# Graph attention layers of a GNN and expert kernel: masks by ScalarE ahead of the first layer, logit sums by half tiles, GpSimd's low parts behind each head

## The reference

```python
def gat_layer(x, W, att_src, att_dst, bias, src, dst, heads, out_ch, concat):
    h = (x @ W.T).reshape(n, heads, out_ch)
    a_src = jnp.einsum('nhc,hc->nh', h, att_src)
    a_dst = jnp.einsum('nhc,hc->nh', h, att_dst)
    e = jax.nn.leaky_relu(a_src[src] + a_dst[dst], 0.2)
    m = jax.ops.segment_max(e, dst, num_segments=n)
    ex = jnp.exp(e - m[dst])
    denom = jax.ops.segment_sum(ex, dst, num_segments=n)
    alpha = ex / (denom[dst] + EPS)
    out = jax.ops.segment_sum(alpha[:, :, None] * h[src], dst, num_segments=n)
    return out + bias
h = gat_layer(x, W1, ..., heads=8, out_ch=128)
out = gat_layer(relu(h), W2, ..., heads=1, out_ch=768)
```

## Time and profile before

| | |
|---|---|
| median of 3 runs | 1395.59 us (1395.35, 1395.59, 1403.01) |
| the profiled execution's own time | 1399.6 us |
| its span | 1397.6 us |
| mean granted TensorE clock | 0.95 |
| busy: PE, PEld, DVE, ACT, POOL | 1248.6, 1063.9, 922.0, 578.2, 133.5 us |
| TensorE's share of the span | 89% |

### The profile page before, as it was taken

The page is one execution under the profiler, slowest core; times in us unless marked ns, Lnnn a source line. Parts: engine busy times, 40 slices in busy tenths (PEclk is TensorE's granted clock), DMA queues, the critical chain, the costliest instruction groups (busy, mean ns, idle before and its releaser), DMA issues.

```text
span 1397.6 us, 18195 instructions
## 1 busy us (share of the span) xinstructions
PE 1248.6 (89%) x6471; PEld 1063.9 (76%) x6471; DVE 922.0 (66%) x1765; ACT 578.2 (41%) x1005; POOL 133.5 (10%) x127
## 2 busy tenths in 40 slices
PE   5999999999999899998788999999985867878876
PEld 3577579879889786657788999999984667765643
DVE  4478664375365564556659999999987679647313
ACT  2121232432522423353148889888871255211110
POOL 0000200000000000033020000000020185010101
PEclk9999999999999999998699999999998979988799
DMA  9420280501402600040468999999984000020286
GB/s 343 146 91 30 102 305 12 204 0 47 169 1 86 232 0 0 1 158 0 147 238 308 386 392 394 382 399 387 386 307 180 27 1 1 1 79 1 100 302 229
DMA packets 82907, 229.72 MB, mean 164 GB/s; under 512 B 5217, under 2 KB 18593, under 8 KB 82721
## 3 DMA queue, kind: packets, MB, share of 16 engines
q1 hardware_dynamic: 74944, 191.96, 37.2%
q0 software_dynamic: 7904, 36.97, 7.2%
HBM read 202.18 MB, written 26.74 MB: 164 GB/s over the span
## 4 chain that ended last, share of the span: by engine, by line
PE 73%; DVE 14%; DMA 5%; issue 3%; ACT 2%; POOL 2%; SPq 0%; ACTq 0%; DVEq 0%; POOLq 0%
PE dve_ps L727 11%; PE dve_ps L729 11%; PE dve_ps L728 11%; PE act_ps L727 4%; PE act_ps L729 4%; PE act_ps L728 4%; PE dve_ps L770 4%; PE dve_ps L816 3%; DMA slot<-in_e1w 2%; PE dve_ps L960 2%; PE act_ps L943 2%; PE act_ps L767 2%; PE act_ps L816 1%; PE dve_ps L1202 1%; DVE part_slot L2100 1%
## 5 line engine op out<-in xcount | busy, mean ns | idle before, releaser
L2091 DVE TENSOR_TENSOR part_slot<-slot,item_hi 128x768 fp32r<-128x768 f32 x150 | 133.5, 957 | 0.4 <-ACT item_hi L1541 0.2
L1541 ACT ACTIVATE item_hi<-slot 128x768 fp32r<-128x768 f32 x156 | 118.0, 834 | 27.8 <-DMA slot<-in_e0w 23.2
L2100 DVE TENSOR_TENSOR part_slot<-slot,item_hi 128x768 fp32r<-128x768 f32 x132 | 116.6, 954 | 0.4
L1549 ACT ACTIVATE item_hi<-slot 128x768 fp32r<-128x768 f32 x132 | 99.3, 833 | 9.0 <-DMA slot<-in_e0w 9.0
L727 PE MATMUL dve_ps<-item_hi,x_hi 128*128 128x384 f32 x288 | 98.8, 343 | 4.1 <-DVE part_slot L2091 2.7
L727 PE MATMUL act_ps<-item_hi,hid_hi 128*128 128x384 f32 x288 | 98.8, 343 | 4.0 <-DVE hid_lo L2292 4.0
L728 PE MATMUL act_ps<-part_slot,hid_hi 128*128 128x384 f32 x288 | 98.0, 340 | 0.0
L729 PE MATMUL dve_ps<-item_hi,x_lo 128*128 128x384 f32 x288 | 97.8, 340 | 0.0
L729 PE MATMUL act_ps<-item_hi,hid_lo 128*128 128x384 f32 x288 | 97.8, 339 | 0.0
L728 PE MATMUL dve_ps<-part_slot,x_hi 128*128 128x384 f32 x288 | 97.7, 339 | 0.0
L1432 ACT ACTIVATE h_t<-act_ps,par 128x256 f32<-128x256 f32 x36 | 21.1, 587 | 121.0 <-PE act_ps L834 121.0
(11 more groups left out here) (398 smaller groups left out, 3254.1 us busy)
## 6 DMA issues: line engine op xcount, KB each, us to landing
slot<-in_e0w SPq DMA_DIRECT2D x48, 2304.0 KB, 10.3
slot<-in_w SPq DMA_DIRECT2D x9, 2304.0 KB, 9.6
slot<-in_e1w SPq DMA_DIRECT2D x12, 1152.0 KB, 6.2
ea_raw<-in_edge SPq DMA_DIRECT2D x8, 1024.0 KB, 5.4
slot<-in_wqkv SPq DMA_DIRECT2D x3, 2304.0 KB, 15.0
xs<-zrow POOLq DMA_DIRECT2D x2, 3072.0 KB, 15.7
ys<-item_y POOLq DMA_DIRECT2D x16, 384.0 KB, 6.7
slot<-in_gw SPq DMA_DIRECT2D x4, 1536.0 KB, 8.5
```

What stands on the lines that cost most here:

```text
L1541: go(item_hi[j][k][:, :], slot[s][:, k * D:(k + 1) * D], ACT.Copy).then_inc(up_high[j], 1)
L1549: go(item_hi[j][k][:, :], slot[s][:, k * D:(k + 1) * D], ACT.Copy).then_inc(down_high[j], 1)
L2091: vv.tensor_tensor(part_slot[s][:, ks], slot[s][:, ks], item_hi[j][k][:, :].bitcast(F32), ALU.subtract).then_inc(up_low[j], 1)
L2100: vv.tensor_tensor(part_slot[s][:, ks], slot[s][:, ks], item_hi[j][k][:, :].bitcast(F32), ALU.subtract).then_inc(down_low[j], 1)
```

## The change

The masks. TensorE turns `ct` into the four `act_ps` banks as soon as the rows are taken, ahead of the features' turning, and waits for ScalarE, which makes the mask by a Relu of 1e30 - 1e30*count (so the mask is 1e30 where there is no edge, and the front subtracts it). The stage "mask" is gone from the ring's numbers. Four of the high parts of the first layer's weights lay where `mask` is, and move to other places; one wait of ScalarE for TensorE goes with that.

The sums. VectorE makes the logit sums of a half tile as soon as that half is there; in the last half the source sums come first and raise `att_set`, on which TensorE spreads. The second layer's last source sum does the same.

GpSimd. In heads 0 and 8 (`SHARED`) it makes only two of four sums, and VectorE the other two behind its front. The low parts of the second layer's weights come one behind each head's sums.

Tables. Three one-column activations on an unused tile stand where ScalarE's set changes next: Gelu behind the first gate's exponential, Exp ahead of the second layer's high parts, Gelu behind head 8.

```diff
-    ("xt2", 3, 3), ("h1", 4, 4), ("mask", 0, 4), ("gat1", 0, GH * 3), ("o1t", 4, 4), ("h2", 4, 4),
+    ("xt2", 3, 3), ("h1", 4, 4), ("gat1", 0, GH * 3), ("o1t", 4, 4), ("h2", 4, 4),
...
-            [4608 * s + 3072 + N * j for s in range(2) for j in range(3)] + [cpt_at + N * j for j in range(4)]
-            + [area + 20480, area + 20480 + N])]
+            [4608 * s + 3072 + N * j for s in range(2) for j in range(3)]
+            + [area + at for at in (17472, 18944, 21504, 22016, 20480, 20992)])]
...
+        SHARED = (0, GH)
+
+        def pool_sums(g):
+
+            return NT * g - 2 * sum(1 for s in SHARED if s < g)
...
             pe.wait_ge(rows_taken, 8)
+            for t in range(NT):
+                for m in range(NT):
+                    turned = nc.tensor.transpose(act_ps[t][:, m * P:(m + 1) * P], ct[:, m, t * P:(t + 1) * P], ident[:, :])
+                turned.then_inc(mask_turned, 1)
+            pe.wait_ge(mask_set, NT)
             turn_features(xn2, ACT0["xt2"], DVE0["xt2"], NT * (L + 2))
...
-            for t in range(NT):
-                bank = dve_bank(t, DVE0["mask"])
-                for m in range(NT):
-                    last = nc.tensor.transpose(bank[:, m * P:(m + 1) * P], ct[:, m, t * P:(t + 1) * P], ident[:, :])
-                last.then_inc(sig.to_dve, 1)
...
             go(prob[:, :, :], logit[:, :, :], ACT.Exp).then_inc(prob_exp, 1)
+            go(table[:, 0:1], ident[:, 0:1], ACT.Gelu)
...
-                elif i == 6:
-
-                    act.wait_ge(down_used[1], DC * last + 2)
                 go(gw1_hi[i][:, :], slot[i // DC][:, i % DC * N:(i % DC + 1) * N], ACT.Copy).then_inc(gw1_high, 1)
+
+            act.wait_ge(const_set, 3)
+            for t in range(NT):
+                act.wait_ge(mask_turned, t + 1)
+                go(mask[:, t, :], act_ps[t][:, :], ACT.Relu, bias=big[:, 0:1], scale=NONE).then_inc(mask_set, 1)
...
+            act.wait_ge(sig.to_act, ACT0["gat1"])
+            act.wait_ge(sig.to_dve, DVE0["gat1"])
+            go(table[:, 0:1], ident[:, 0:1], ACT.Exp)
             for k in range(GD // P):
                 ks = slice(k % 4 * D, (k % 4 + 1) * D)
                 go(part_slot[k // 4][:, ks], slot[2 + k // 4][:, ks], ACT.Copy).then_inc(w_high, 1)
...
                 for t in range(NT):
-                    act.wait_ge(g_sum, NT * g + t + 1)
+                    if g in SHARED and t >= 2:
+                        act.wait_ge(g_sum_dve, 2 * SHARED.index(g) + t - 1)
+                    else:
+                        act.wait_ge(g_sum, pool_sums(g) + t + 1)
...
             graph_exps(GH)
+            go(table[:, 0:1], ident[:, 0:1], ACT.Gelu)
...
             for t in range(NT):
-                bank = bank_of(t, DVE0["h1"])
-                vv.tensor_copy(h1x[:, t, 4:8, 0:GC], bank[:, :].rearrange("p (h c) -> p h c", h=4)).then_inc(sig.dve_freed, 1)
-
-                dve.wait_ge(sig.act_freed, ACT0["h1"] + t + 1)
-                dve.wait_ge(sig.dve_freed, DVE0["h1"] + t + 1)
-                settle()
-                for which in range(2):
-                    then(vv.tensor_tensor(by_head(scr[:, which, :]), h1x[:, t, :, 0:GC], by_head(att1[:, which, :]), ALU.mult))
-                settle()
-                for which in range(2):
-                    then(vv.tensor_reduce(att[:, which, t, :], by_head(scr[:, which, :]), AX_X, ALU.add))
+                for half in range(2):
+                    hs = slice(4 * half, 4 * half + 4)
+                    if half == 0:
+                        dve.wait_ge(sig.act_freed, ACT0["h1"] + t + 1)
+                    else:
+                        bank = bank_of(t, DVE0["h1"])
+                        vv.tensor_copy(h1x[:, t, hs, 0:GC], bank[:, :].rearrange("p (h c) -> p h c", h=4)).then_inc(sig.dve_freed, 1)
+                        dve.wait_ge(sig.dve_freed, DVE0["h1"] + t + 1)
+                    settle()
+                    for whichs in ((0,), (1,)) if u_last(t, half) else ((0, 1),):
+                        for which in whichs:
+                            then(vv.tensor_tensor(by_head(scr[:, which, :])[:, hs, :], h1x[:, t, hs, 0:GC], by_head(att1[:, which, :])[:, hs, :],
+                                                  ALU.mult))
+                        settle()
+                        for which in whichs:
+                            last = vv.tensor_reduce(att[:, which, t, hs], by_head(scr[:, which, :])[:, hs, :], AX_X, ALU.add)
+                            if u_last(t, half) and which == 0:
+                                last.then_inc(att_set, 1)
+                            else:
+                                then(last)
...
-            for t in range(NT):
-                bank = bank_of(t, DVE0["mask"])
-                vv.tensor_scalar(mask[:, t, :], bank[:, :], 0.0, NONE, ALU.is_equal, ALU.mult).then_inc(sig.dve_freed, 1)
-            dve.wait_ge(sig.dve_freed, DVE0["gat1"])
-            dve.wait_ge(att_set, 1)
+            dve.wait_ge(att_set, 2)
+            dve.wait_ge(mask_set, NT)
...
-                                            op0=ALU.add, op1=ALU.max, accum_out=gmax[:, b, t:t + 1]).then_inc(g_masked, 1)
+                                            op0=ALU.subtract, op1=ALU.max, accum_out=gmax[:, b, t:t + 1]).then_inc(g_masked, 1)
...
                 vv.tensor_tensor(gdec[:, b, 2, :], a_dst, gdec[:, b, 1, :], ALU.subtract).then_inc(g_dec, 1)
+                if g in SHARED:
+                    for t in range(2, NT):
+                        dve.wait_ge(g_bent, NT * g + t + 1)
+                        vv.tensor_tensor(raised[:, b, t, :], raised[:, b, t, :], masked[:, b, t, :], ALU.add).then_inc(g_sum_dve, 1)
...
-            for k in range(GD // P):
-                ks = slice(k % 4 * D, (k % 4 + 1) * D)
-                low_of(2 + k // 4, ks, part_slot[k // 4][:, ks], k)
-
             for g in range(GH + 1):
-                for t in range(NT):
+                for t in range(2 if g in SHARED else NT):
                     pool.wait_ge(g_bent, NT * g + t + 1)
                     one = raised[:, g % 2, t, :]
                     nc.gpsimd.tensor_tensor(one, one, masked[:, g % 2, t, :], ALU.add).then_inc(g_sum, 1)
+                if g < GD // P:
+                    ks = slice(g % 4 * D, (g % 4 + 1) * D)
+                    low_of(2 + g // 4, ks, part_slot[g // 4][:, ks], g)
```

30 lines of the change are left out of this document (20 added, 10 removed).

## The result

| | before | after | after, again |
|---|---|---|---|
| median | 1396.99 us (6 runs) | 1387.69 us (6 runs, 1381.76 to 1390.24) | 1390.94 us (12 runs, 1382.19 to 1394.18), beside before 1399.73 |
| ratio to before, 95% interval | | 0.9917 (0.9898 to 0.9936) | 0.9930 (0.9903 to 0.9958) |
| profiled execution, its span | 1399.6, 1397.6 us | 1389.16, 1387.6 us | 1390.93, 1389.4 us |
| mean granted clock | 0.95 | 0.952 | 0.952 |
| busy PE, DVE, ACT, POOL | 1248.6, 922.0, 578.2, 133.5 | 1248.7, 922.2, 579.5, 128.2 | |

The ratios with their intervals are worked out from the single runs; the quotients of the medians are 0.9933 and 0.9937. The forecast was 1385.1 (1380.5 to 1390.5), the class "within 1%". The median lies within the range, and the class is right. By the ratios the gain is 0.7 to 0.8%. Busy times are almost the same; what changed is where the waits lie.

What follows compares the result with a forecast made beforehand. Graph attention's entry was bound by VectorE's sums and masks and GpSimd's low parts, from head 3 by VectorE. Gains 7.3+1.3+1.9 = 10.5 us took the profiled 1399.6 to 1389.1; less 4 for the median, 1385.1 (1380.5 to 1390.5).

Steps and rivals of the forecast that it cites:

- sum of 10.5 us: Whole kernel: gains of 7.3 (graph attention entry), 1.3 (Gelu table) and 1.9 us (second layer) added up.
- Way in: First graph attention layer's entry up to head 3's front: 7.3 us gained, ends 6.3 and 8.2.
- Low parts, 0: GpSimd's low parts, one behind each head: VectorE's reciprocal and weights not held, 0 us lost.
- bound of 4 us: Upper bound on loss if low parts hold VectorE's reciprocal: up to 0.7 us each, six times.
- Gelu, 1.3: First expert Gelu: its table load moves behind the gate's exp, 1.3 us gained, bounds 0 and 1.3.
- Second layer, 1.9: Second layer's entry: earlier spread and shared sums let exps start at 1250.55; 1.9 us gained, bounds 1.0 and 2.5.
- The masks warm TensorE: Rival, chance 0.20: mask transposes raise the clock before the features' turning, 2.4 us more gained, 1382.7 us.
- Small terms go: Rival, chance 0.14: head 0 entry gains 6.3, Gelu 0, second layer 1.0; 7.3 us in all, 1388.3 us.
- Low parts holding VectorE: Rival, chance 0.04: low parts block VectorE's weights or outputs 2.0 us in seven periods, 14 us lost, 1399.1 us.
- masks not hidden: Rival, chance 0.02: mask transposes or Relus end behind 1071.6, all after slips, 2 us at worst, 1387 us.

Runs made afterwards that it cites:

- after, again: The changed kernel measured once more as it is, beside the kernel before: median 1390.94 us, ratio to before 0.9930.
- nothing shared: Changed kernel with GpSimd making all four sums of head 0 and of the second layer, VectorE none: 1389.78 us, ratio to before 0.9921.
- masks late: Changed kernel with VectorE making the masks behind the logit sums, from transposes behind the products, as before: 1389.63 us, ratio to before 0.9924.

## Why the prediction was right, and where it was not

The sum of 10.5 us stands against 10.0 between the two profiled executions, 9.3 between the medians and 8.8 in the repeat. The 10.0 agrees so well by luck: 2.6 us lost and 2.6 us won lie in stretches that the change does not explain. The parts with an edit behind them add up to 9.7. Of the 2.6 us between forecast and median, 1.4 come from the starting point, since the median of before rose from 1395.59 in three runs to 1396.99 in six.

*Way in, 7.3 us.* Right: 7.5. The points, forecast and measured: masks ahead of the features (they ended 0.6 us later than forecast, at 1071.52, since all stands 0.7 later here, and what TensorE waited for was VectorE's normalising); front 0 at 4.0 and 3.9; bends at 1118.6 and 1118.81 with ScalarE late for head 0; VectorE's wait ahead of its first shared sum about 2 and 2.27; TensorE's output of head 0 done at 1139.4 and 1139.73; front 1 at 1123.1 and 1123.06; front 3 at 30 and 29.74. The alternation of VectorE and GpSimd at head 0, taken from the 2.84 us of a held operation, came out as 2.37 us for two sums. That the sum was right doesn't make each part of the change right: the prediction wrote that head 1's front is queued behind the shared sums, but never asked what the way in would be without them. It would have been 1.8 to 2.5 us shorter, as two runs showed, 1.9 of them apart from the clock.

*Low parts, 0.* Right. The reciprocal beside GpSimd took 0.18 us and the period is 9.1. Of the bound of 4 us nothing came. The Trainium skill (SBUF — State Buffer, Who interferes with whom) says that a VectorE instruction with at most one SBUF input, outside the two-port modes, does not contend with GpSimd, and that one with two does where GpSimd reads SBUF. The trace agrees here: the reciprocal with one input wasn't held, while `gdec` with two took 1.19 and 1.72 us.

*Gelu, 1.3.* Right as far as it can be read: 62.91 to 61.45 us, 1.5 locally.

*Second layer, 1.9.* The mechanism was right, and early by 2.2 us up to the exps. The step that failed is the unspoken one behind it, that TensorE's work keeps its length when it starts sooner. It started at a granted clock of 0.50 where before it had 1.00, and lost 1.55. Net 0.64, which lies below the prediction's lower bound of 1.0. In the changed kind this is the rule: in all eight profiles of it without filler the weighted sums took 17.3 us or more, and the clock stood at 0.50 at their start or within their first three microseconds. That the earlier start is the reason is not shown. The kernel before was profiled once, and its 15.79 us may be the luck of that execution: with nothing shared, TensorE turned the weights as far behind the spread as in the kernel before (7.5 us), and the sums took longest of all, 18.73.

*The masks warm TensorE (chance 0.20).* Not in the first profile, where the turning started at 0.50. But it did in the changed kernel's second profile, and in three of its variants without filler. This is the changed kernel, again:

```profile
1074.25 0.31 PE L719 MATMUL act_ps<-ident,xn 128*128 128x128 f32 x1 [1.85 <-DVE xn L1792]
```

The same transposes that cost 0.45 and 0.42 us in the first profile cost 0.31 and 0.27 here. Of seven profiles with the masks ahead and no filler it happened in four, in one more for half of the turning, and in two not at all; the two without masks ahead (before, masks late) both started at 0.50. N was 39.4 instead of 40.9 to 41.3. So in these profiles the rival came in about one of two, not one of five; it came in all three profiles of the chip of the repeats, and in one and the half of the other four, so that the share may depend on the chip. Against the kernel before it is worth 1.8 us (N from 41.23 to 39.40) of the 2.4 forecast: the turning fell from 5.2 us to 2.8, but TensorE then waited 0.96 us for VectorE ahead of the first product instead of 0.57. Against the first profile it is 1.5, since there the clock rose within the turning, which took 4.3. The Trainium skill (TensorE: Matmul & The Clock Gate, Part 1) says that where the rise falls varies between runs. The traces agree, 0.45 and 0.31 us for the same transpose of one program.

*The other rivals.* Small terms go (1388.3): of its three terms (6.3, 0 and 1.0) the third alone came, for another reason than the one given; the first two were 7.5 and 1.5. The median of 1387.69 lies nearer to this rival's time than to the forecast's, and only the distances tell them apart. Low parts holding VectorE, and masks not hidden: neither.

## What to carry to other kernels

Work given to a second engine to relieve a first is paid in the second's queue: look at what stands behind it there, and share only where nothing does (here the last layer, not head 0). A gain of 1 or 2 us ahead of a stretch of TensorE work can be hidden by the clock at which that work starts; read the granted clock of the stretch that follows, and try keeping TensorE busy in its waits, which in twelve more places was worth 9.7 us here, about as much as the whole change. And where runs of one program lie 12 us apart, measure a part of 2 us by the distance of two instructions in several profiles, and end it ahead of TensorE's work where the clock can change its length.

## What the runs showed of the hardware

- The same wait (2.57 us) and the same transposes behind it ran at either level of the clock, 0.66 or 1.11 us for four; filler in the waits kept the level at 2.4 GHz in most of the places read (0.66 us behind 18 transposes, 15.79 us for the weighted sums in four profiles of four), but not behind the first gate (0.57 from 678 to 682 us) and not in the second (0.50 from 1262).
- A ScalarE table load cost 1.28 us and the dummy behind it 0.2, of which the next instruction hid half; nothing else was seen of it.
- VectorE's small operations on two SBUF inputs took 0.16 us alone, 1.19 beside a GpSimd sum of 1.24 us, and 1.72 to 1.74 beside a GpSimd low part of 1.8 us. Two sums of 128x512 took 1.28 us alone and 2.37 where GpSimd made two of its own beside them, which took 2.99 instead of 2.5.
